# Three-term f32r products in the token preparation, and an early first stack for the attention behind it

## The reference, cut to what matters

```python
qkv = jnp.einsum('bld,ed->ble', x, w_qkv)
q, k, v = jnp.split(qkv, 3, axis=-1)          # then (B, L, H, Dh)
q = _rope(q)
k = _rope(k)
scores = jnp.einsum('blhd,bmhd->bhlm', q, k) * scale
attn = jax.nn.softmax(scores, axis=-1)
out = jnp.einsum('bhlm,bmhd->blhd', attn, v).reshape(B, L, D)
```

## Time and profile before

| what | us |
|---|---|
| median of three runs | 2305.58 |
| the runs | 2305.26, 2305.58, 2310.74 |
| profiled execution, its own time | 2310.06 |
| its span | 2308.3 |
| TensorE busy in the span | 2197.8 (95%) |
| VectorE busy | 1620.2 (70%) |
| ScalarE busy | 1375.1 (60%) |
| GpSimd busy | 614.2 (27%) |

### The profile page before, as it was taken

The page is one execution under the profiler, slowest core; times in us unless marked ns, Lnnn a source line. Parts: engine busy times, 40 slices in busy tenths (PEclk is TensorE's granted clock), DMA queues, the critical chain, the costliest instruction groups (busy, mean ns, idle before and its releaser), DMA issues.

```text
span 2308.3 us, 43409 instructions
## 1 busy us (share of the span) xinstructions
PE 2197.8 (95%) x14592; PEld 1287.6 (56%) x14592; DVE 1620.2 (70%) x3785; ACT 1375.1 (60%) x2547; POOL 614.2 (27%) x493
## 2 busy tenths in 40 slices
PE   7869999999999987989999999999999999999998
PEld 4533333334333335656766766756766766766755
DVE  5767999999999936666566665656666665655635
ACT  2214888888888864645655645645655645655633
POOL 4521300000000005423333333323333233333302
PEclk9975999999999998999999999999999999999999
DMA  4575111122211112210000000000010000000122
GB/s 139 181 236 173 57 57 57 56 66 66 66 47 57 43 63 94 95 37 1 1 0 0 0 0 0 27 1 1 9 37 1 1 0 0 0 0 0 55 92 73
DMA packets 76984, 108.96 MB, mean 47 GB/s; under 512 B 14204, under 2 KB 49360, under 8 KB 76752
## 3 DMA queue, kind: packets, MB, share of 16 engines
q1 hardware_dynamic: 76864, 107.30, 14.6%
HBM read 68.74 MB, written 43.95 MB: 49 GB/s over the span
## 4 chain that ended last, share of the span: by engine, by line
PE 51%; DVE 2%; issue 1%; ACT 1%; DVEq 0%; ACTq 0%
PE ffn L1199 24%; PE l_ps_o L1157 5%; PE ring L1145 5%; PE ring L1185 4%; PE ps_v L1132 3%; PE ps_q L1132 3%; PE ps_k L1132 2%; PE ring L1169 2%; PE ring L1187 1%; DVE l_probs L1675 1%; PE ring L1188 0%; ACT k_ring L1481 0%; DVE l_probs L1687 0%; ACT l_probs L1489 0%; PE ps_k L1221 0%
## 5 line engine op out<-in xcount | busy, mean ns | idle before, releaser
L669 DVE TENSOR_REDUCE maxima<-ps_m 128x1 f32<-128x512 f32 x1024 | 629.7, 683 | 30.7 <-PE ps_m L549 26.7
L737 ACT ACTIVATE probs<-ps_st 128x1024 f32<-128x1024 f32 x512 | 521.0, 1025 | 172.0 <-PE ps_st L576 152.8
L549 PE MATMUL ps_m<-k_st,q_st 48*128 48x512 f32 x1024 | 398.2, 472 | 19.8 <-DMA k_st<-ks 15.6
L576 PE MATMUL ps_st<-q_st,k_st 50*128 50x512 f32 x1024 | 373.3, 450 | 2.3 <-DMA q_st<-max_rows 1.9
L1489 ACT ACTIVATE l_probs<-l_probs,l_neg_max 128x256 f32<-128x256 f32 x512 | 254.0, 498 | 194.8 <-DVE l_neg_max L1675 194.8
L592 PE MATMUL ps_o<-probs,v_st 128*32 128x256 f32 x4096 | 327.4, 398 | 0.1
L1675 DVE CUSTOM_DVE_ANT_1 l_probs<-ring,l_mask 128x256 f32<-128x256 f32 x384 | 140.1, 421 | 198.5 <-PE ring L1185 198.0
L576 PEld LDWEIGHTS ps_st<-q_st,k_st 50*128 50x128 f32 x1024 | 157.2, 189 | 198.4 <-issue 176.5
L1468 ACT COPY p_turned<-ring 128x512 f32<-128x512 f32 x256 | 140.4, 599 | 163.7 <-PE ring L1145 163.5
L1094 POOL TENSOR_SCALAR clipped<-sumsq 128x16 f32<-128x16 f32 x64 | 16.1, 252 | 765.7 <-DVE sumsq L1642 765.7
L549 PEld LDWEIGHTS ps_m<-k_st,q_st 48*128 48x128 f32 x1024 | 169.4, 193 | 53.0 <-DVE maxima L669 31.3
(11 more groups left out here) (192 smaller groups left out, 3879.7 us busy)
## 6 DMA issues: line engine op xcount, KB each, us to landing
qs<-split SPq DMA_DIRECT2D x16, 512.0 KB, 3.5
ks<-split SPq DMA_DIRECT2D x16, 512.0 KB, 5.1
q_st<-qs SPq DMA_DIRECT2D x64, 128.0 KB, 2.5
k_st<-ks SPq DMA_DIRECT2D x64, 128.0 KB, 3.2
o<-o_sb SPq DMA_DIRECT2D x32, 256.0 KB, 2.4
hidden<-o SPq DMA_DIRECT2D x17, 256.0 KB, 6.5
x_in<-in_L_attn_x_dram SPq DMA_DIRECT2D x8, 512.0 KB, 5.6
v<-v_sb SPq DMA_DIRECT2D x16, 256.0 KB, 4.7
```

Of the source, the lines that this page charges most:

```text
L549: nc.tensor.matmul(bank(base, use)[:, :], q_st[u][r, qt * P:(qt + 1) * P], k_st[u][r, h * CH:(h + 1) * CH], start=True, stop=True).then_in ...
L576: mm = nc.tensor.matmul(ps_st[j][:, h * CH:(h + 1) * CH], k_st[u][r, kt * P:(kt + 1) * P], q_st[u][r, h * CH:(h + 1) * CH], start=True, st ...
L669: nc.vector.tensor_reduce(maxima[:, par, side(e), tile + e // 4, e % 2:e % 2 + 1], bank(base, k + e)[:, :], AX_X, ALU.max).then_inc(m_used, 1)
L737: nc.scalar.activation(probs[:, kt % 4, j, :], ps_st[j][:, :], ACT.Exp, scale=float(G_DIM) ** -0.5).then_inc(exp_done, 1)
```

## The change

1. The products of the first block are made of three f32r terms: high x high, high x low and low x high, over both halves k (`TERMS3`, six passes where two f32 products stood). The weights are split once at the start: ScalarE writes `w_parts[0]`, VectorE `w_parts[1]`; TensorE starts behind that. x is split for each half: ScalarE copies a turned half from PSUM twice, to `xnt` and rounded to `xs[0]`, and VectorE subtracts (`x_low`). GpSimd's copy to `xnt` is gone but for one column.
2. `turn_x` and `take_x` of the next batch's half 0 stand behind tile 6 instead of 7; `x_low` stands ahead of the rotations of tiles 3 and 7.
3. The first pair of stacks gets memory of its own, which lives through all three blocks (the third uses it for its `h`). It is filled by GpSimd at the first block's start and loaded by SyncE during that block, behind the stores of batch 1.
4. The other three fills are GpSimd's too, one over the whole of a key stack, at the second block's start. `k_ones` counts one a stack.
5. `store` sends the values first, then queries and keys.

```diff
+    def set_ones(self, pool, u):
+        self.nc.gpsimd.memset(self.k[u][:, :].bitcast(F32), -1.0).then_inc(self.ones, 1)
+
+    def load(self, sp, i, u, first=False):
+        qs_dram, ks_dram = self.dram
+        for j in range(2):
+            head, at = 2 * u + j, self.BLOCK * j
+            src = qs_dram[bass.ds(i, 1), head, :, :, :].rearrange("o d s n -> (o d s) n")
+            sp.dma_start(self.q[u][at:at + self.PAIRS, :].bitcast(F32), src).then_inc(self.arrived[u], 16)
+            if first:
+
+                sp.wait_ge(self.ones, u + 1)
...
@@ prepare_tokens
+        w_parts = [w[:, :, 0:3 * D] for w in wt.wqkv]
-        xs = sb("xs", [P, 2, KD, CH])
+        xs = [sb("xs_high", [P, 2, KD, CH], F32R), wt.w1[0][:, :, 0:2 * CH].rearrange("p k (c n) -> p c k n", c=2)]
+        TERMS3 = [(k, a, b) for k in range(KD) for a, b in ((0, 0), (0, 1), (1, 0))]
@@ sync: store(i, c)
+                    sp.wait_ge(v_copied, 8 * i + 4 * c + 4)
+                    for f in range(KD):
+                        dst = v_dram[bass.ds(2 * i + f, 1), c * 4:c * 4 + 4, :, :].rearrange("o t p n -> p (o t) n")
+                        sp.dma_start(dst, v_sb[:, c, :, f * P:(f + 1) * P]).then_inc(stored[c], 16)
                     sp.wait_ge(low_done, 8 * i + 4 * c + 4)
...
@@ sync: behind the loop over batches 0 and 1
+                for c in range(2):
+
+                    sp.wait_ge(stored[c], 16 * STORES)
+                stacks.load(sp, 0, 0, True)
@@ gpsimd
-                        pool.wait_ge(xs_done, 4 * i + 2 * c + 2)
-                        apart(pool, pool_passed)
-                        for k in range(KD):
-                            nc.gpsimd.tensor_copy(xnt[:, k, bass.ds(2 * i + c, 1), 1:].rearrange("p o n -> p (o n)"),
-                                                  xs[:, c, k, :]).then_inc(xnt_done, 1)
...
+                stacks.set_ones(pool, 0)
                 body(0, False)
@@ vector
+                def x_low(i, c):
+                    for k in range(KD):
+                        dve.wait_ge(xs_high, 4 * i + 2 * c + k + 1)
+                        src = xnt[:, k, bass.ds(2 * i + c, 1), 1:].rearrange("p o n -> p (o n)")
+                        nc.vector.tensor_tensor(xs[1][:, c, k, :], src, xs[0][:, c, k, :], ALU.subtract).then_inc(xs_done, 1)
+
                 def body(i, first, last):
+                    if first:
+                        x_low(i, 0)
                     for t in range(TILES):
+                        if t == 3:
+                            x_low(i, 1)
+                        if t == TILES - 1 and not last:
+                            x_low(i + 1, 0)
                         rotate(i, t, first)
...
+                for k in range(KD):
+                    dve.wait_ge(w_high, k + 1)
+                    nc.vector.tensor_tensor(w_parts[1][:, k, :], wqkv[:, k, :], w_parts[0][:, k, :], ALU.subtract).then_inc(w_low, 1)
@@ scalar
                     for k in range(KD):
-                        nc.scalar.copy(xs[:, c, k, :], ps_x[k][:, :]).then_inc(xs_done, 1)
+                        nc.scalar.copy(xnt[:, k, bass.ds(2 * i + c, 1), 1:].rearrange("p o n -> p (o n)"), ps_x[k][:, :]).then_inc(xnt_done, 1)
+                        nc.scalar.copy(xs[0][:, c, k, :], ps_x[k][:, :]).then_inc(xs_high, 1)
...
-                        if t == TILES - 1 and not last:
+                        if t == TILES - 2 and not last:
                             take_x(i + 1, 0, False)
@@ tensor
-                    for k in range(KD):
-                        mm = nc.tensor.matmul(ps_qk[t % 2][:, :], xs[:, c, k, s], wqkv[:, k, 0:2 * D], start=(k == 0), stop=(k == KD - 1))
+                    for n, (k, a, b) in enumerate(TERMS3):
+                        mm = nc.tensor.matmul(ps_qk[t % 2][:, :], xs[a][:, c, k, s], w_parts[b][:, k, 0:2 * D], start=(n == 0), stop=(n == len(TERMS3) - 1))
...
+                pe.wait_ge(w_low, KD)
                 body(0, True, False)
@@ global_attention, sync
-                for u in range(NB):
-                    load(0, u, True)
-                    if u == 0:
-                        sp.dma_start(ident[:, :], ident_in).then_inc(ident_loaded, 16)
+                sp.dma_start(ident[:, :], ident_in).then_inc(ident_loaded, 16)
+                for u in range(1, NB):
+                    stacks.load(sp, 0, u, True)
@@ global_attention, gpsimd and vector
+                for u in range(1, NB):
+                    stacks.set_ones(pool, u)
...
-                for u in range(NB):
-                    for j in range(2):
-                        nc.vector.memset(k_st[u][BLOCK * j + PAIRS:BLOCK * (j + 1), :].bitcast(F32), -1.0).then_inc(k_ones, 1)
@@ local_layers
-        h = [sb(f"h_{n}", [P, KD, CH], F32R) for n in ("high", "low")]
+        h = [rows.rearrange("p (k n) -> p k n", k=KD) for rows in (stacks.q[0], stacks.k[0])]
```

More of the change, by code:

```diff
@@ L270, in body @@
                                        ps_t[t % 2][:, :].rearrange("p (f n) -> p f n", f=4)).then_inc(high_done, 1)
+                act.wait_ge(consts_in, 48)
+                for k in range(KD):
+                    nc.scalar.copy(w_parts[0][:, k, :], wqkv[:, k, :]).then_inc(w_high, 1)
                 body(0, True, False)
@@ L294, in project @@
                         pe.wait_ge(v_copied, 8 * i + t - 1)
-                    for k in range(KD):
-                        mm = nc.tensor.matmul(ps_qk[t % 2][:, :], xs[:, c, k, s], wqkv[:, k, 0:2 * D], start=(k == 0), stop=(k == KD - 1))
+                    for n, (k, a, b) in enumerate(TERMS3):
+                        mm = nc.tensor.matmul(ps_qk[t % 2][:, :], xs[a][:, c, k, s], w_parts[b][:, k, 0:2 * D], start=(n == 0), stop=(n == len(TERMS3) - 1))
                     mm.then_inc(qk_mm, 1)
-                    for k in range(KD):
-                        mm = nc.tensor.matmul(ps_v[t % 2][:, 0:D], xs[:, c, k, s], wqkv[:, k, 2 * D:], start=(k == 0), stop=(k == KD - 1))
+                    for n, (k, a, b) in enumerate(TERMS3):
+                        mm = nc.tensor.matmul(ps_v[t % 2][:, 0:D], xs[a][:, c, k, s], w_parts[b][:, k, 2 * D:], start=(n == 0), stop=(n == len(TERMS3) - 1))
                     mm.then_inc(v_mm, 1)
@@ L340, in global_attention @@
         NB = 4
-        BLOCK, PAIRS, TERMS, ROWS = 4 * G_DIM, 2 * G_DIM, 3 * G_DIM, 3 * G_DIM + 2
+        BLOCK, PAIRS, TERMS, ROWS = stacks.BLOCK, stacks.PAIRS, stacks.TERMS, stacks.ROWS
         ident = sb("g_ident", [P, P])
-        q_st, k_st = zip(*[[sb(f"{n}_st{u}", [2 * BLOCK, L], F32R) for n in "qk"] for u in range(NB)])
+        for u in range(1, NB):
+            stacks.add(ctx)
+        q_st, k_st, qk_in, k_ones = stacks.q, stacks.k, stacks.arrived, stacks.ones
         maxima = sb("maxima", [P, 2, 2, TILES, 2])
@@ L364, in global_attention @@
         v_ones = sem("v_ones")
-        k_ones = sem("k_ones")
-        qk_in = [sem(f"qk_in{u}") for u in range(NB)]
         v_loaded = sem("v_loaded")
@@ L462, in body @@
                             sp.wait_ge(st_ready, 2 * TILES * (NB * i + u) + 2 * TILES)
-                            load(i + 1, u)
+                            stacks.load(sp, i + 1, u)
                     if last:
```

59 lines of the change are left out of this document (33 added, 26 removed).

## The result

The changed kernel takes 2338.12 us (median of four runs, 2334.76 to 2362.19); the kernel before took 2305.42 beside it. The ratio is 1.0162, 95% interval 1.0125 to 1.0199: slower by 1.6%, where 2294.6 was forecast and the range ended at 2308. The profiled execution took 2335.77 us with a span of 2333.6.

The account below looks back on a forecast made before the run. TensorE was taken as nearest to the bound in the first stage, VectorE close behind. First stage 3 plus handover 8 gave 11 us off the profiled 2310.06, 2299; for the median 2294.6 us was predicted, range 2284 to 2308.

Parts of the forecast that it names:

- D: Rival, first stage: TensorE falls to the low clock and stays there; 2320 us for two batches, 2346 for all; chance 0.07.
- First stage: Token preparation: first product at 21.1 us, VectorE becomes the busier engine, stage ends at 132.55 instead of 137.98; 3.0 gained after deductions.
- allowances: First stage: deductions of 0.4 us a batch for scaling under GpSimd's sum and 1.2 for one fall of the clock.
- The rule on weight loads: First stage, counter-estimate: a 128-column load takes about 0.107 us, so a tile costs 3.65 us instead of the forecast 2.60.
- F: Rival, first stage: VectorE's sixteen low halves of x each wait out a GpSimd sum, 20 us lost, 2315; chance 0.05.
- Handover: First block to attention: fewer stack loads start the raw copies 8.4 us sooner and the first scores 8 sooner; bounds 6 and 11.
- E: Time when the first stage's last low half ends, from which handover times are counted; 137.98 us in the kernel before.
- C': Rival, attention's first unit: the full clock returns inside it, up to 14.7 us more gained, 2280 to 2292; chance 0.07.
- C: Rival, attention: the full clock returns a unit later, sixteen half steps cost 14.7 us, 2309.3; chance 0.10.

Follow-up runs that it names:

- e7: Changed kernel with eight tiny VectorE fills ahead of its attention loop, which then starts at instruction 406: 2294.20 us, ratio 0.9960.
- e13: Kernel before with four tiny VectorE fills ahead of its attention loop, which then starts at instruction 388: 2340.67 us, ratio 1.0154.
- e14: Changed kernel with four tiny VectorE fills ahead of its attention loop, which then starts at instruction 402: 2350.13 us, ratio 1.0195.
- e10: e7 with one VectorE operation of 2.64 us added at the top of the loop over groups of four units: 2341.72 us, ratio 1.0136.
- e8: e1 with SyncE issuing the raw weight copies behind the first row maxima instead of ahead of them: 2297.38 us, ratio 0.9974.
- e1: Changed kernel with 32 tiny VectorE fills ahead of its attention loop, which then starts at instruction 430: 2295.81 us, ratio 0.9957.
- e2: Kernel before with 14 tiny VectorE fills ahead of its attention loop, which then starts at instruction 398: 2342.13 us, ratio 1.0161.
- e5: Changed kernel with VectorE's loop over the groups of four units written out, no fills added: 2293.86 us, ratio 0.9955.
- e12: e5 with the raw weight copies behind the first row maxima, and SyncE's wait for them and following weight loads behind the second unit's rows: 2289.70 us, ratio 0.9933.

## Why the prediction was wrong

**The step that failed** is in its first paragraph: "Behind that only the place of one pair of buffers changes, and I price it at nothing". The place of the code changed too, by 14 instructions on VectorE. I counted the eight fills that go and the subtractions that come by their durations, and not by what they do to what stands behind them. No rival held it either. D had the right kind of loss, TensorE at its low clock, in the wrong stage: the first stage has a clock of 1.00 from its first product on. The price of the failed step is 2338.12 - 2294.20 (e7) = 43.9 us by the medians. The profiled execution has 43.4; that the two agree so closely is luck, since the changed kernel's runs are 27 us apart.

**The mechanism, as far as the runs show it.** A load is 8.2 KB. The Trainium skill, "Vector Engine (DVE) Microarchitecture Reference", section "Instruction fetch and dispatch (NX sequencer)", gives an instruction 64 bytes; by that estimate a load has 128. A loop of 276 = 2 x 128 + 20 lies in three loads, or in four if it starts in one of some 20 places of 128 (19; 21 if its two waiting instructions hold places too). The bad starts 388 to 402 and the good ones 384 and 406 bound a stretch of 15 to 21 places, and 526 repeats 398: that fits, and e13 and e14 were forecast from it. That a loop over four loads has to be loaded again and one over three has not is what the counts of 63 and 38 agree with; how the chip keeps them, and where in memory a load begins, is not shown. The Trainium skill, "Runtime: NRT & Kernel Launch", section "Instruction fetch mechanics", says that a taken branch whose target is outside the loaded window forces a load before execution goes on. The stops agree in kind (2 to 3 us at the jumps). Its blocks of 256 instructions do not agree: a load is half of that here, and with such blocks a loop of 276 would have one bad stretch of some 20 places in 256, so that 398 and 526, 128 apart, could not both be bad.

A stop of 2 to 3 us would be bearable. It costs nearly four times as much (43.4 us against 12.0 of stops), because VectorE reduces two products in 1.24 us while TensorE's half step is 1.23, so that nothing is made up, and because the clock falls behind the pause: 5 to 15 us at a place. e10 shows this apart from code loading. One stop brought no fall (at 437.7, 2.1 us lost). How much time the falls take differs between executions, and that is the changed kernel's spread of 27 us: its four runs have a mean granted clock of 0.962, 0.962, 0.959 and 0.950, the last in the slowest, and the span times the clock is 2242 to 2245 us in all four. In e7 that product is 2240 to 2241, so by this estimate some 40 of the 44 us are low clock.

**First stage.** Right. First product 21.85 (21.1 forecast; VectorE's second scaling took 2.24 us instead of 1.51, with GpSimd's fill of a stack beside it, which may be the cause, and the weight lows end at 16.94 instead of 16.15). Batches 28.6, 27.9, 27.7 and 27.4 (starts 50.45, 78.33, 106.02) against 28.3, 27.6, 27.6 and 27.95; the wait at a batch's start 1.56 against 1.5. VectorE is the busier engine, 24.7 us of a batch (24.8 forecast). The 256-column pass takes 0.12, its lower bound. 4.5 us gained lies between the 5.4 of the sum and the 3.0 after allowances, of which the fall of the clock did not come. The rule on weight loads of the Trainium skill, "TensorE: Matmul & The Clock Gate", section "LDWEIGHTS (loading the stationary operand)", that would have made a tile 3.65 us does not hold here at full clock: 0.23 and 0.12 from start to start, each with a load of its own. F did not come either: the sixteen subtractions of x took 0.69 in the median and 1.22 at most.

**Handover.** The order of events was right, its size not: 4.9 us instead of 8, 43.0 behind E instead of 39.6. Two terms were too small. The raw copies start at E + 19.8, not + 18.3: the 24 loads took 14.5, but begin at E + 4.9, behind a load of `g_ident`, and a load of values stands behind them. The prediction's sum had lost these two: 34 issues less eight are 26, at 0.59 each 15.3 us, and its 14.3 is 24 of them. And from the raw copies to the scores are 23.2 us, not 21.3. The wait for the rows is 4.81 (4.5 forecast). That the raw copies' queue decides is shown by e8: without them ahead, the wait is gone, though the rows are issued no sooner (161.57 against 161.23 in e1).

**Clock in the first unit.** C' came, in the profiled execution: the clock is back after 12 us instead of some 38, and the unit takes 26.7 us instead of 37.3, worth 10.6. It is no effect of the change. Of kernels without stops, e7 had it back at 187 (span 2288.7) and e1 at 213 (span 2298.8), and they differ by 24 tiny fills; the kernel before with fills had it back after 14 us (e2) and 10 (e13). Single runs of before spread over 2298 to 2314 likewise, one at 2322, with mean granted clocks from 0.977 down to 0.965. So a single execution is uncertain by 10 us, and the medians of ten runs by some 4, by their intervals. C's price per half step was 2.16 from 35 us over sixteen, which is 2.19; the traces have 2.16 (e8, 176.81 to 178.97).

**The sum.** Without the stops the change is worth 9.1 to 10.7 us (e1, e5, e7 against before) where 11 was forecast, and 2293.9 to 2295.8 where 2294.6 stood. That the total is so near is partly luck: the first stage gave 4.5 instead of 3 and the handover 4.9 instead of 8, and the two errors go opposite ways.

## What to carry to other kernels

Every instruction that is added or removed ahead of a loop moves the loop's code. For an engine that jumps back in the hot part, count its instructions before and after, and look in the trace for idle time put down to "issue" at the jumps and for a count of instruction loads that has risen. If it has, write the loop out or shift it, before anything of the change itself is judged: here 8 idle fills were worth 44 us, and the change some 10. And when a queued transfer is moved, follow what stands behind it on its queue: the gain of e8 was lost one unit later to a wait which e12 moves too.

## What the runs showed of the hardware that was not expected

- A loop of 276 VectorE instructions costs stops of 2.0 to 3.0 us at jumps back when it starts on instruction 388, 398, 402 or 526, and none at 376, 384, 406, 430 or 438. Instruction loads are 8.2 KB: 63 or 64 in the bad kernels, 38 or 39 in the good ones.
- Written out, the same work has no stop and 43 loads.
- Six pauses of TensorE, 1.9 us at most and 11.1 us in all, came with a loss of 47.5 us in e10 (by the medians), most of it by the fall of its clock: a run's mean granted clock is 0.953 to 0.966 there and 0.977 to 0.979 in e7.
- f32r products of 256 columns start 0.12 us apart, of 512 columns 0.23, with a weight load each, at full clock; at the low clock 512 columns are 0.43 apart (22.44 to 24.15).
